# Two conditioned layers on one core: VectorE's first variances ahead of centering, and GpSimd's power ahead of both low halves of h

## What is computed

```
# layer 0: the kind c is 0 (NR), 1 (TSR) or 2 (SR)
out_nr  = gelu(x @ w1_nr  + b1_nr)  @ w2_nr  + b2_nr
out_tsr = gelu(x @ w1_tsr + b1_tsr) @ w2_tsr + b2_tsr
out_sr  = gelu(gelu(x @ w1_sr + b1_sr) @ w2_sr + b2_sr) @ w3_sr + b3_sr   # inner width 512
z  = x + (out_nr, out_tsr, out_sr or 0, by kind)
y  = (z - mean(z)) * rsqrt(var(z) + EPS) * gamma + beta        # the first norm
# layer 1: one of 16 experts e
h  = gelu(y @ down_W.T + down_b)
u  = y + (h @ expert_W[e].T + expert_b[e] + domain_emb[e]) @ up_W.T + up_b
out = (u - mean(u)) * rsqrt(var(u) + EPS) * ln_gamma + ln_beta # the second norm
```

## Time and profile before

| what | value |
|---|---|
| median of 3 runs | 270.54 us (270.42 to 270.87) |
| the profiled execution | 270.59 us, of which the trace's span is 268.8 us |
| busy share of the span: PE, DVE, ACT, POOL | 94%, 78%, 71%, 66% |
| SR steps | to about 105 us |
| two-layer steps | about 105 to 248 us |

### The profile page before, as it was taken

One profiled execution on the slowest core, in us unless ns is written; L12 is line 12 of the kernel. 1 busy time (PEld: TensorE's weight loads), 2 busy tenths in 40 slices (PEclk: granted clock), 3 DMA queues, 4 the chain that ended last, 5 costly groups with the idle time before them and its releaser, 6 DMA issues.

```text
span 268.8 us, 8023 instructions
## 1 busy us (share of the span) xinstructions
PE 251.5 (94%) x2114; PEld 220.7 (82%) x2115; DVE 208.9 (78%) x717; ACT 191.2 (71%) x450; POOL 177.4 (66%) x188
## 2 busy tenths in 40 slices
PE   7998999999999998899999999999999999999970
PEld 6698898999999987788888888888788898888640
DVE  6769643474774674899999998998898989898894
ACT  3578479578678676687777777778687877778650
POOL 3134374463776775877777778777878787878551
PEclk9999999999999999999999999999999999999996
DMA  6372011011112112133332323323232322322315
GB/s 200 86 261 62 12 41 43 4 42 41 43 41 78 39 39 78 41 92 82 88 85 81 93 82 87 88 78 87 78 89 80 95 78 78 98 79 69 76 44 121
DMA packets 41639, 20.71 MB, mean 77 GB/s; under 512 B 37430, under 2 KB 39180, under 8 KB 41613
## 3 DMA queue, kind: packets, MB, share of 16 engines
q1 hardware_dynamic: 37625, 12.10, 18.6%
q0 software_dynamic: 2592, 7.08, 7.5%
q10 hardware_dynamic: 1396, 1.19, 1.7%
HBM read 11.69 MB, written 8.65 MB: 76 GB/s over the span
## 4 chain that ended last, share of the span: by engine, by line
PE 43%; DVE 17%; issue 15%; POOL 10%; ACT 7%; DVEq 4%; DMA 1%; ACTq 0%; POOLq 0%
PE ps_h L1089 14%; POOL h_lo L482 6%; PE ps_t L1179 5%; PE ps_z L1162 5%; POOL rs L489 4%; PE ps_z L1157 4%; DVE st L691 3%; PE ps_u L1209 3%; DVE n L727 3%; DVEq L338 2%; PE ps_t L1260 2%; PE ps_z L1124 2%; ACT yt L937 2%; DVE o L767 2%; PE ps_t L1263 2%
## 5 line engine op out<-in xcount | busy, mean ns | idle before, releaser
L482 POOL TENSOR_TENSOR h_lo<-h,h_hi 128x256 fp32r<-128x256 f32 (+1 forms) x75 | 73.3, 978 | 37.6 <-ACT h L903 35.1
L489 POOL TENSOR_TENSOR rs<-ve,minus_half 128x4 f32<-128x4 f32 (+1 forms) x38 | 38.2, 1005 | 31.6 <-DVE ve L703 31.4
L910 ACT ACTIVATE zn<-ps_z,nm,rs 128x256 f32<-128x256 f32 x66 | 33.7, 560 | 32.9 <-DVE nm L707 27.7
L691 DVE BATCH_NORM_STATS2 st<-ps_z 128x6 f32<-128x256 f32 x66 | 24.8, 415 | 32.7 <-PE ps_z L1162 32.7
L903 ACT ACTIVATE h_hi<-ps_h,per_feature_sb 128x256 fp32r<-128x256 f32 x84 | 38.6, 492 | 10.2 <-PE ps_h L1089 6.0
L937 ACT ACTIVATE yt<-ps_t,per_feature_sb 128x256 f32<-128x256 f32 x66 | 34.0, 573 | 10.1 <-PE ps_t L1179 9.6
L903 ACT ACTIVATE h<-ps_h,per_feature_sb 128x256 f32<-128x256 f32 x84 | 38.7, 498 | 0.0
L508 POOL DMA_INDIRECT out<-o,out_rows_now x27 | 34.2, 1267 | 4.7 <-issue 4.7
L1209 PE MATMUL ps_u<-tables,stack 65*64 x132 | 35.5, 392 | 0.3 <-ACT stack L921 0.3
L1209 PE MATMUL ps_u<-second_table,stack 65*64 65x256 f32 x132 | 35.6, 392 | 0.0
L1157 PE MATMUL ps_z<-last_hi,h_hi 128*128 (+1 forms) x132 | 35.4, 304 | 0.0
(11 more groups left out here) (150 smaller groups left out, 657.6 us busy)
## 6 DMA issues: line engine op xcount, KB each, us to landing
x<-in_x_feat SPq DMA_DIRECT2D x130, 64.0 KB
out<-o SPq DMA_DIRECT2D x18, 64.0 KB, 2.2
out<-o,out_rows_now POOLq DMA_INDIRECT x54
last_sb<-in_last_w SPq DMA_DIRECT2D x1, 768.0 KB, 5.1
w_sr_sb<-in_w_sr SPq DMA_DIRECT2D x1, 512.0 KB, 3.3
w_sr_sb<-in_w_sr ACTq DMA_DIRECT2D x1, 512.0 KB, 4.5
w_two_sb<-in_w_two SPq DMA_DIRECT2D x1, 512.0 KB, 5.7
out<-o ACTq DMA_DIRECT2D x6, 64.0 KB, 2.3
```

What stands on the lines that cost most here:

```text
L482: pool.tensor_tensor(dst, full, high.bitcast(F32), ALU.subtract).then_inc(ready, 1)
L489: pool.tensor_tensor(RS[p][:, norms, :], VE[p][:, norms, :], half_of_two[:, norms, :], ALU.pow).then_inc(rstd, 1)
L910: ins = act.activation(ZN[:, t, :], ZP[p][:, t, :], ACT.Identity, bias=NM[p][:, t:t + 1], scale=RS[p][:, 0, t:t + 1])
```

## The change

Two orders are changed; no instruction is added or removed.

```diff
@@ GpSimd, the branch for two-layer steps
                 with pool.Else():
+                    powers(g, i, p, where)
                     for slot in on_slot(g, -1, where):
                         low(h2l[:, 0, :], h2[:, 0, :], h2h[:, 0, :], h0_full, h0_lo, g + 1)
-                    powers(g, i, p, where)
-                    for slot in on_slot(g, -1, where):
                         low(h2l[:, 1, :], h2[:, 1, :], h2h[:, 1, :], h1_full, h1_lo, g + 1)
@@ VectorE, every step but LAST1, LAST0 and DRAIN
                 for slot in on_slot(g, 0, where):
                     first_stats(slot, p)
-                for slot in on_slot(g, 3, where):
-                    center(slot, q, p)
                 for slot in on_slot(g, 0, where):
                     first_moments(slot, p)
                 variances(p, BOTH)
+                for slot in on_slot(g, 3, where):
+                    center(slot, q, p)
                 for slot in on_slot(g, 2, where):
                     second_stats(slot, p)
```

## The result

The changed kernel takes 278.5 us (median of 4 runs, 277.84 to 278.81) against 270.54 us. The ratio is 1.030, with a 95% interval of 1.0275 to 1.0321. The direction was forecast, the size was not: +8.0 us against +3.35, outside the range of 271.0 to 276.6.

The account below looks back on a forecast made before the run. TensorE was taken to bound SR steps, a ring through VectorE, GpSimd, TensorE and ScalarE the two-layer steps. Terms of +2.4, +0.25, +0.3 and +0.4 gave +3.35 on 270.59: 273.9 us, range 271.0 to 276.6.

Parts of the forecast that it names:

- The gain of the early variances: Two-layer steps: without centering in between, statistics to `ve` take 1.20 us instead of 1.71, a gain of 0.51 us.
- Low0 on the path: Two-layer steps: low0 leaves GpSimd's idle time for between power and low1, costing 0.73 us; L1162 starts net 0.21 later.
- The collision: Two-layer steps: x_lo and a low exclude each other; x_lo follows low0, ahead of low1; 6.28 us a step, 50%.
- rival one: Two-layer steps: low1 goes straight behind low0 and x_lo waits for both; 6.40 us a step, 276.3 us in all, 20%.
- The forecast step of 6.15: First step of a two-layer pair: x_lo, held by low0 until 3.08, goes ahead of low1; 6.15 us against 5.94.
- The long step of 6.40: Second step of a two-layer pair: low1 holds x_lo until 3.80; the step of 6.38 us becomes about 6.40.
- LAST1: At the end, low0 stands ahead of low1, +0.73 us, of which 0.13 to 0.73 is left; taken as 0.4.
- The transition: The two steps from 105.7 to 117.6 us have the same collision, at about 0.15 us each: +0.3.
- the last SR step: At the end of the SR steps TensorE waits for VectorE's bias, and VectorE is later by 0.25 us: +0.25.
- Nothing in the SR steps: SR steps: no loss, since TensorE is the bound and GpSimd's order doesn't change there.
- the edit's 0.25 us on VectorE: VectorE's wait for the statistics, formerly covered by centering: 0.25 us taken, costing nothing because TensorE's u still comes last.
- The rule of the Trainium skill: VectorE against GpSimd on SBUF: issue order decides who blocks, so x_lo, asked for at 2.87, precedes low1, at 3.20.

Follow-up runs that it names:

- after_power_held: The changed kernel, with GpSimd's power in SR steps made to wait, ahead of the low, for VectorE's centering: 275.07 us, ratio 1.019.

## Why the prediction was right in the two-layer steps and wrong in sum

**The gain of the early variances** was priced at 0.51 us, and is 1.18 against 1.71: 0.53. Right.

**Low0 on the path** was priced at 0.73, net 0.21 later. The trace of the changed kernel has the power at 1.44, low0 at 2.47 and L1161 at 4.38, and the halves tried apart give +0.5 to +0.6 for GpSimd's and -0.4 to -0.5 for VectorE's. TensorE's loads behind low1 waited 8.8 us for h_lo in the 20 steps, where they had waited 6.3. Right as a mechanism, and it is GpSimd's half that costs. The prediction didn't see that the other half by itself would win 0.38 us a step.

**The collision**, x_lo behind low0 and ahead of low1, was taken over rival one (behind both). Shown by the pair of lows of 1.86 us. The forecast step of 6.15 came out at 6.13. The long step of 6.40 came out at 6.35, and the mean at 6.24 against 6.28: +1.6 us instead of +2.4. Without the SR loss the whole would have come to +2.7 us, which has the forecast sign and lies inside the range; so the sign is not owed to that loss.

**The smaller terms.** LAST1 took 5.14 us instead of 4.83: +0.31 against 0.4; another 0.18 came behind it. The transition took +0.61 against 0.3, and the last SR step +0.10 against the 0.25 that was put there.

**The step that failed** is the sentence "Nothing in the SR steps: TensorE is the bound, and GpSimd's order doesn't change there." Both halves of it are true, and the conclusion is not. VectorE's order does change there, and this moves GpSimd's power and low, which wait for `ve`, by half a microsecond. I had put the edit's 0.25 us on VectorE at nothing, because TensorE's u came last; that cover was read in a two-layer step, and an SR step doesn't have it: there the second statistics start without a wait, at 1.82 before and at 2.11 in the changed kernel. And I took an engine that is idle for 38% of a stage to have slack. It has it in sum, but x_lo was made 0.06 us before TensorE read it. What the runs show in its place is 0.28 us of later asking, worth 0.3 us a step, and 0.85 us because the low now came first and held x_lo: 1.14 us in each of the four steps of 11.2 us, and 0.1 us in the last, 4.6 in all. The term should have been +4.6 instead of +0.25; with it the sum would have been 278.3 us, with the two-layer steps still 0.8 too high in it and the transition 0.3 too low. Two runs bracket it: after_power_held, which removes the second part, keeps 1.5 us of the loss, and dve_sr_only, VectorE's half in SR steps alone, has the whole, 4.7 us.

**The rule of the Trainium skill** that was weighed, page "SBUF — State Buffer", section "Who interferes with whom", has it that the issue order decides who blocks. It held in both places, with 1.86 us for the lows in the two-layer steps and 1.52 us for x_lo in the SR steps. An estimate from the SR rows of the kernel before gives the loss: with the prediction's own shifts of 0.25 and 0.51 us x_lo is asked for at 2.75 and the low at 2.50; the low, 1.28 us long in the changed kernel's row, would free x_lo 0.12 before its end, at 3.66, and x_lo would end at 4.33 instead of 3.17. That is 1.16 us a step, and 4.6 for four steps. I had set the two starts against each other in the other stage only.

## What to carry to other kernels

When an edit moves the release of another engine's work, redo the race for every shared resource in every stage that runs the code, also in a stage with another bound: two starts 0.5 us apart had changed order here, and that was worth more than all the intended moves. Ask of each result who reads it next and how long before, not how idle its maker is. And try the halves of an edit apart: here one half won 1.2% (1.9% with SR steps left mostly alone), and the other cost 3 to 5%. When a profiled run is to explain a step that is out of line, look at the granted clock of that step too.

## What the runs showed of the hardware beyond what was expected

A VectorE instruction of two elements a partition is held by a low just as a long one: `nm` took 0.52 us instead of 0.12 behind x_lo in the changed kernel's short steps, and 1.09 beside the 128x512 low in the SR steps of the kernel before. Of two GpSimd lows queued back to back, the second let a waiting x_lo go first, each time (1.86 us for the pair, in every second step). GpSimd's issue of an indirect store took 2.48 to 2.61 us instead of 1.2 to 1.4 in the two kernels that held the SR low back until x_lo was made; what held it was not tried.
